# Two attentions with heads of eight numbers: scores of f32r parts in half of TensorE's rows, slots filled from SBUF

## The reference, cut to what matters

```python
# a1, causal
scores = einsum('bhqd,bhkd->bhqk', q, k) / sqrt(8)
scores = where(causal, scores, -inf)
o = einsum('bhqk,bhkd->bhqd', softmax(scores), v)      # then @ W_proj + b_proj
# b1, encoder: no mask, no scale, and a position bias that is added after the softmax
att = softmax(einsum('nqd,nkd->nqk', q, k))
att_out = einsum('nqk,nkd->nqd', att + batch_pos, v)   # then @ Wo.T + bo
```

## Time and profile before

| | us |
|---|---|
| three runs | 2855.39, 2871.22, 2868.68; median 2868.68 |
| profiled execution, its own time | 2866.75 |
| its span, first to last instruction | 2864.9 |
| its mean granted TensorE clock | 0.907 of 2.4 GHz |

### The profile page before, as it was taken

How to read it: one execution, slowest core, us unless ns; L and a number is a source line. 1 busy time by engine, 2 the same in 40 slices (tenths; PEclk the granted TensorE clock), 3 DMA queues, 4 the chain that set the end, 5 groups by cost and what they waited for, 6 DMA issues and landing times. The chain is left out here.

```text
span 2864.9 us, 41721 instructions
## 1 busy us (share of the span) xinstructions
PE 2471.5 (86%) x12332; PEld 1460.6 (51%) x12332; DVE 2117.8 (74%) x4148; ACT 1425.9 (50%) x3005; POOL 645.5 (23%) x621
## 2 busy tenths in 40 slices
PE   6994899939988999779996499999758899969998
PEld 4772344327756555457773422222125555437776
DVE  3994767538968999279995188788337899738998
ACT  2552356615520787246664036666611387615665
POOL 2334000013328000124444100000004500013443
PEclk7996799969979999889997769999978999979999
DMA  1213222012210000034442621211121000004443
GB/s 64 81 55 74 52 60 60 20 47 95 75 41 5 1 1 1 8 115 153 142 151 46 155 44 28 53 29 28 24 30 41 5 1 1 8 6 157 144 152 117
DMA packets 109527, 169.58 MB, mean 59 GB/s; under 512 B 58547, under 2 KB 80947, under 8 KB 98275
## 3 DMA queue, kind: packets, MB, share of 16 engines
q1 hardware_dynamic: 92468, 165.47, 19.5%
q10 hardware_dynamic: 16896, 2.10, 0.5%
HBM read 145.96 MB, written 12.78 MB: 55 GB/s over the span
## 5 line engine op out<-in xcount | busy, mean ns | idle before, releaser
L1483 DVE TENSOR_REDUCE b1x_maxima<-b1x_m_bank 128x1 f32<-128x512 f32 x512 | 317.9, 685 | 79.1 <-PE b1x_m_bank L1401 79.1
L1523 ACT ACTIVATE b1x_probs<-b1x_e_bank 128x1024 f32<-128x1024 f32 x256 | 248.3, 1022 | 117.4 <-PE b1x_e_bank L1419 117.2
L1483 DVE TENSOR_REDUCE a1x_maxima<-a1x_m_bank 128x1 f32<-128x512 f32 (+3 forms) x384 | 190.1, 551 | 73.1 <-PE a1x_m_bank L1404 49.3
L1401 PE MATMUL b1x_m_bank<-b1a_k_slot,b1a_q_slot 96*128 96x512 bf16 x512 | 190.8, 413 | 19.2 <-DMA b1x_v_slot<-b1a_v_aug 18.5
L1523 ACT ACTIVATE a1x_probs<-a1x_e_bank 128x1024 f32<-128x1024 f32 (+1 forms) x192 | 147.7, 809 | 102.4 <-PE a1x_e_bank L1422 80.1
L1419 PE MATMUL b1x_e_bank<-b1a_q_slot,b1a_k_slot 128*128 128x512 bf16 x512 | 154.1, 385 | 6.5 <-issue 3.9
L1435 PE MATMUL b1x_o_bank<-b1x_probs,b1x_v_slot 128*32 128x512 f32 x1024 | 137.4, 609 | 0.7 <-ACT b1x_probs L1523 0.7
L1401 PE MATMUL a1x_m_bank<-a1a_k_slot,a1a_q_slot 96*128 96x512 bf16 (+3 forms) x384 | 120.5, 351 | 19.9 <-DMA a1x_v_slot<-a1a_v_aug 18.6
L1401 PEld LDWEIGHTS b1x_m_bank<-b1a_k_slot,b1a_q_slot 96*128 96x128 bf16 x512 | 41.6, 98 | 177.2 <-DVE b1x_maxima L1483 126.2
L585 ACT ACTIVATE g1e_high<-g1e_hidden 128x512 fp32r<-128x512 f32 x128 | 81.1, 634 | 90.2 <-DVE g1e_hidden L618 90.1
L585 ACT ACTIVATE g2e_high<-g2e_hidden 128x512 fp32r<-128x512 f32 x128 | 81.2, 634 | 89.8 <-DVE g2e_hidden L618 89.6
(11 more groups left out here) (556 smaller groups left out, 6616.0 us busy)
## 6 DMA issues: line engine op xcount, KB each, us to landing
g1e_share<-scratch_combine SPq DMA_DIRECT2D x32, 1024.0 KB, 4.9
g2e_share<-scratch_combine SPq DMA_DIRECT2D x32, 1024.0 KB, 4.8
f1e_share<-scratch_combine SPq DMA_DIRECT2D x9, 1024.0 KB, 4.9
f2e_share<-scratch_combine SPq DMA_DIRECT2D x9, 1024.0 KB, 5.0
b1e_window<-scratch_bias_table SPq DMA_DIRECT2D x16, 320.0 KB, 4.8
a1a_k_slot<-scratch_k_parts SPq DMA_DIRECT2D x24, 192.0 KB
a1a_q_slot<-scratch_q_parts SPq DMA_DIRECT2D x72, 64.0 KB
b1a_k_slot<-scratch_k_parts SPq DMA_DIRECT2D x24, 192.0 KB
```

The lines of the kernel that those rows point to most:

```text
L1401: mm = pe.matmul(bank[:, 0:width], q_slot[s][0:MAX_ROW, qt // 4, hh, chunk(qt % 4, 128)], k_slot[s][0:MAX_ROW, hh, k0:k0 + width], start=T ...
L1483: dve.tensor_reduce(maxima[:, k0 // NC, col:col + 1], bank[:, 0:width], AX, ALU.max).then_inc(m_taken, 1)
L1523: act.activation(probs[g % 2][:, 2 * pair:2 * pair + 2, 0:width], e_bank[pair][:, :, 0:width], ACT.Exp, scale=scale).then_inc(exp_done, 1)
```

## The change

- Parts: two f32r parts (high, rest) instead of three bf16. A head takes 24 rows (q: high, rest, high; k: high, high, rest), zeros in q up to row 55, and the maximum's two parts in rows 56 and 57 against ones. Two heads lie in the two halves of the rows (0 and 64), two pairs beside each other in the free dimension. First-pass matmuls take 56 rows, second-pass scores 58, from row 0 or 64. Items run over the heads innermost, and the second pair's scores in the order 1, 0. The mask matmuls stay as they were (128 rows).
- Cutting: ACT writes the high part (one activation), DVE the rest (one scalar_tensor_tensor). No part goes to DRAM. `load` fills a slot with 2 x 4 x 3 DMAs from SBUF: groups 0 and 1 in earlier phases (a1: SP in q and in w; b1: SP in d, ACT's queue in e), group 2 at the start of x, later ones behind. The values are read from `v_aug` in place.
- POOL sets whole slots (k to 1.0, q to 0.0) in q, ahead of `v_aug`.
- Groups are unrolled. A plan `due(u)` gives the m items per unit by their columns; all turns stand six items behind their half. The rows' DMAs are 4 a half instead of 3, one half ahead (encoder) or two (causal).
- The encoder's q and k weights are permuted, so that a part's partition is (number, position).

The diff, cut to its core:

```diff
-PARTS = 3
+PARTS = 2
-MAX_ROW = 96
+MAX_ROW = 56
+SLOTS = 3
@@ class Narrow
+    ROW_PARTS = {"q": (0, 1, 0), "k": (0, 0, 1)}
+    LOADED = 16 * 2 * 4 * 3
+    def load(self, queue, group, operand):
+        parts, slot = ((self.q_parts, self.q_slot) if operand == "q" else (self.k_parts, self.k_slot))
+        s = group % SLOTS
+        for e in range(4):
+            b, n = (4 * group + e) // NH, (4 * group + e) % NH
+            for i, part in enumerate(self.ROW_PARTS[operand]):
+                if self.positions_split:
+                    src = parts[:, part, b * L + 64 * n:b * L + 64 * n + 64]
+                else:
+                    src = parts[HD * n:HD * n + HD, part, chunk(b, L)]
+                r = 64 * (e % 2) + HD * i
+                queue.dma_start(slot[s][r:r + HD, e // 2, :].bitcast(F32), src.bitcast(F32)).then_inc(self.slot_loaded[s], 16)
+    def prepare_slots(self, pool):
+        for s in range(SLOTS):
+            self.memset(pool, self.k_slot[s][:].bitcast(F32), 1.0)
+            self.memset(pool, self.q_slot[s][:].bitcast(F32), 0.0)
@@ qkv_in_parts: SP (a1), POOL, ACT, DVE
+                sp.wait_ge(narrow.set, 2)
+                sp.wait_ge(low_done, 4)
+                narrow.load(sp, 0, "q")
+                narrow.load(sp, 0, "k")
+            narrow.prepare_slots(pool)
             narrow.prepare_values(pool)
+                    act.activation(parts[m][:, 0, chunk(n)], acc[i % ROT][:], ACT.Identity,
+                                   bias=b[:, m:m + 1]).then_inc(high_done, 1)
+                dve.scalar_tensor_tensor(out=parts[m][:, 1, chunk(n)], in0=acc[i % ROT][:],
+                                         scalar=b[:, m:m + 1], in1=parts[m][:, 0, chunk(n)],
+                                         op0=ALU.add, op1=ALU.subtract).then_inc(low_done, 1)
@@ narrow_attention: the plan
+    for half in reversed(range(HALVES)):
+        items.insert(min(last_item[half] + 6, len(items)), (half, None))
+    AHEAD = 2 if causal else 1
+    worth = [0]
+    for item in items:
+        worth.append(worth[-1] + (item[4] + 32 if item[1] is not None else 256))
+    def due(u):
+        if u >= NU:
+            return NI
+        lead = turn_at[AHEAD - 1] + (8 if causal else 12)
+        done, whole = (sum(unit[3] + 32 for unit in units[:u]), sum(unit[3] + 32 for unit in units))
+        aim = worth[lead] + worth[NI] * done / whole
+        return max(m for m in range(NI + 1) if worth[m] <= aim)
@@ SP
+            narrow.load(sp, 2, "q")
+            rows(0)
+            narrow.load(sp, 2, "k")
+            for half in range(1, AHEAD):
+                rows(half)
+            for half in range(HALVES):
+                group = half // 2 + SLOTS - 1
+                if SLOTS <= group < GROUPS and half % 2 == 0:
+                    sp.wait_ge(pv_done, last_unit[half - 1] + 1)
+                    narrow.load(sp, group, "q")
+                    narrow.load(sp, group, "k")
+                if half + AHEAD < HALVES:
+                    rows(half + AHEAD)
+                store(half)
@@ PE: first_pass, scores
+                rows = slice(64 * (hh % 2), 64 * (hh % 2) + MAX_ROW)
+                mm = pe.matmul(bank[:, 0:width], q_slot[s][rows, hh // 2, chunk(qt, 128)],
+                               k_slot[s][rows, hh // 2, k0:k0 + width], start=True, stop=not diagonal)
                 if diagonal:
                     mm = pe.matmul(bank[:, width - 128:width], ident_bf[:], mask[:, 0, :],
                                    start=False, stop=True)
+                for a in ((0, 1) if pair == 0 else (1, 0)):
+                    rows = slice(64 * a, 64 * a + MAX_ROW + PARTS)
+                    mm = pe.matmul(e_bank[pair][:, a, 0:width], k_slot[s][rows, pair, chunk(kt, 128)],
+                                   q_slot[s][rows, pair, lo:lo + width], start=True, stop=not diagonal)
                     if diagonal:
                         mm = pe.matmul(e_bank[pair][:, a, 0:128], ident_bf[:], mask[:, 1, :],
                                        start=False, stop=True)
```

More of the change, by code:

```diff
@@ L1105, in prepare_values @@
         self.memset(pool, self.v_heads[:, :, :, :, HD], 1.0)
[L1107 to L1115, removed]
 def qkv_in_parts(nc, tag, dram, narrow, h, early, name, v):
     ROT = 6
[L1128 to L1131, removed]
+    items = [(2, n) for n in range(NCH)] if v is not None else []
+    VALUES = len(items)
+    items += [(m, n) for n in range(NCH) for m in range(2)]
     with Phase(nc, tag) as p:
@@ L1267, in narrow_attention @@
         block = p.block()
[L1268 to L1282, removed]
+        heads_out = dram["heads_out"]
         @block.sync
@@ L1372, in _ @@
-            rows(0, 0)
-            def step(it, j, group, last):
-                if not last:
-                    rows(group + 1, (j + 1) % 3)
-            over_groups(pool, step)
-        def count(group, per, index):
-            return group * per + index
+            for half in range(HALVES):
+                into = max_parts[half % 2]
+                pool.wait_ge(m_taken, turn_at[half] + 1)
+                if half >= 2:
+                    pool.wait_ge(rows_set[half % 2], 64 * (half // 2))
+                pool.tensor_copy(into[:, 0, :], rest[:]).then_inc(cut, 1)
+                pool.wait_ge(cut, 2 * half + 1)
+                pool.tensor_tensor(into[:, 1, :], rest[:], into[:, 0, :], ALU.subtract).then_inc(cut, 1)
@@ L1472, in m_item @@
-            def m_item(group, s, m):
-                item = items[m]
-                dve.wait_ge(m_done, count(group, NM, m + 1))
-                bank = m_bank[(s * NM + m) % 3]
-                if item[0] == "turn":
-                    dve.wait_ge(cut, group * (2 * CUT) + item[1] * CUT + CUT)
+            for m in range(NI):
+                half, qt = items[m][0:2]
+                qh = half % 2
+                dve.wait_ge(m_done, m + 1)
+                bank = m_bank[m % 3]
+                if qt is None:
+                    if half >= 1:
+                        dve.wait_ge(cut, 2 * half)
@@ L1543, in _ @@
-            over_groups(act, step)
+            exponentials(0)
+            for u in range(NU):
+                half = units[u][0]
+                if u + 1 < NU:
+                    exponentials(u + 1)
+                if u == last_unit[half]:
+                    act.wait_ge(pv_done, u + 1)
+                    if half >= 2:
+                        act.wait_ge(o_stored[half % 2], 64 * (half // 2))
+                    act.activation(o_sb[half % 2][:], o_bank[:], ACT.Copy).then_inc(o_copied, 1)
```

368 lines of the change are left out of this document (119 added, 249 removed).

## The result

The changed kernel takes 3132.05 us (median of 4 runs, 3127.92 to 3135.48) against 2864.41 of the kernel before beside it: ratio 1.094, interval 1.0909 to 1.097. It is slower, as forecast, but by 268 us and not by 120; the time lies above the range. The profiled execution took 3135.48 us, span 3133.6, 268.7 more than that of before.

The account below looks back on a forecast made before the run. PE (TensorE), busy 86% of the span, was taken to bound the kernel. From 2866.75 us, +202 (a1x), -55 (b1x), -21 and -8 (ahead of them) gave 2985; range 2860 to 3090.

Parts of the forecast that it names:

- The price of a trip: On PE, going between full and half rows and back costs 0.31 us at 2.4 GHz, about 0.44 at 1.2.
- a1x at full clock: Causal attention a1x goes from 285.8 to 403 us (+117), with +159 from 512 trips at the masks.
- The clock in a1x: In a1x a third of the work runs at 1.2 GHz, +85 us, making a1x 488.
- The bound of two thirds: Upper bound for a1x: two thirds at the low clock, +287 us, and 20 more if f32r is slower at 128 columns.
- b1x's unit: In encoder attention b1x, PE needs 2.06 us a unit, under DVE's 2.39; with extras and slack the unit is 2.55.
- The rows in b1x: In five groups of b1x, SP's 24 slot DMAs delay the rows DMAs, costing 8 us.
- Ahead of the stretches: Phases before b1x and a1x shorten, mainly since slots are filled earlier: -21 us and -8 us.
- A: Rival: shape changes are free or hidden, so packing wins everywhere; a1x -53 us, time 2730, chance 0.15.
- C: Rival: half of the trip is hidden and the clock holds; a1x +37 us, time 2820, chance 0.09.
- B: Rival: trips cost 0.31 us but the clock holds through a1x; a1x +117 us, time 2900, chance 0.14.
- D: Rival: the row halves don't run together; b1x's unit is 2.94 us, time 3055, chance 0.02.
- DVE's idle near nothing: Sign in b1x that the forecast is right: DVE hardly idles, with units of 2.5 to 2.6 us.

Follow-up runs that it names:

- experiment 5: Kernel after with each of the 512 causal mask matmuls issued four times in a row, all trips kept: 3069.21 us, ratio 1.0721.
- experiment 7: Kernel after with one first-pass item instead of two ahead of the values, encoder only: 3188.49 us in a single run.
- Experiments 4 and 6: Against the kernel after: 4, rows DMAs ahead of slot loads, 3118.52 us; 6, that plus half-row masks and one unit more encoder lead, 2850.13 us.

## Why the prediction was wrong

The mechanism was right, and so was the sign. The sum missed 150 us: 100 in a1x, 46 in b1x, the rest ahead of them.

- **The price of a trip: right.** 0.32 and 0.40 us for 0.31 and 0.44, and at 2.4 GHz also in its parts: 0.10 and 0.11 for the two changes of shape and 0.11 for a weight load in the open, for 0.09, 0.09 to 0.10 and 0.11 read from the earlier trace rows.
- **a1x at full clock: right.** By the estimate from experiment 5 a group takes 48.7 for 32.0 us, +16.7; the forecast's +117 over eight groups is +14.7. For the whole stretch: the clock's 0.56 means that some 88% of the 587.4 us were at the lower level, where work takes 77.6 / 48.7 = 1.59 times as long, so it would be 517 / 1.59 + 70 = 395 us. The forecast had 403.
- **The clock in a1x: the step that failed.** "With a third of the work at 1.2 GHz ... +85". Measured: 587.4 - 395 = 192 us. Not a third but some four fifths of the work ran at 1.2 GHz (517 / 1.59 = 325 of 395 us, an estimate, since the 48.7 is one). The price for such work was about right: 85 us for a third would be 210 for 0.82 of it. In one group of the trace not a microsecond was at 2.4 GHz. I had expected the clock to come back among the full-width units without masks; it did so for 3.4 to 17 us at a time. The third was a guess about lengths, and no row gave it: the earlier trace rows have a stretch with PE busy 1.90 of 3.40 us ahead of a fall and one with 32.79 of 36.00 at 1.00, but also one with 32.86 of 34.00 at 0.50, so the busy share could not tell which way a1x would go. The bound of two thirds (+287) was passed, and +301.6 is under +307 only by the 20 us for slower f32r, which did not come.
- **b1x's unit:** "PE unit under DVE's 2.39, unit 2.55" assumed that the later of two engines sets the pace. The loop of three banks does, at 2.70 (experiment 7): 117 x 0.15 = 18 us of the 46 to 50 missed. The last item's 0.42 (2005.06 to 2005.48, for 0.21 of columns) belongs to this loop too: its weight load starts only at 2005.06, when its bank is free, so the load lies in the open beside the change of shape.
- **The rows in b1x:** priced at 8 us. Experiments 4 and 6 took out 5 to 13 (rows behind the loads) and about 15 more (the chain from turn to rows was later than the lead in every half, not in five groups). Left is 382.8 against the 352 of the forecast without this term: the unit's 18, a unit of 3.30 at the start of each half, 15 x 0.6 = 9, in which ACT also copies the output bank (read from the order of time, not tested), and 4 that I can't place. The forecast said b1x -55; it was -8.5.
- **Ahead of the stretches: right.** -18.1 and -6.5 for -21 and -8; the slots in SBUF give what they should.
- **The rivals.** A and C are out by the trips, B by the clock, D by the pairs. "DVE's idle near nothing" was a wrong sign to look for.

The forecast's rule on the upper bound was sound, but the range stopped at the sum of a1x's bound and my point values for b1x; b1x's miss carried the time past it.

## What to carry to other kernels

Here packing paid only once everything that is interleaved had the packed shape: bring masks, biases and transposes into it (here twice 64 rows for once 128) before counting the gain. Price the clock as a state of a whole stage, at both levels, and don't read it from the busy share. After a change that makes a stage faster, look again at each queue that feeds it: the same order on SP was free at 72 us a group and cost 35 us in all at 33.

## What the runs showed that I had not expected

- More matmuls took less time twice: 1536 matmuls added to the kernel after, -63 us (3132.05 to 3069.21); 1024 added to the kernel without masks, a1x from 307.6 to 295.7.
- PE's clock stood at 1.2 GHz for 77.6 us while the profile showed PE busy for 99.5% of it. The Trainium skill, "TensorE: Matmul & The Clock Gate", section HAM oscillation, lays such a fall to gaps in which PE idles; PE's only wait in this stretch was 0.4 us, so here that is not enough as an explanation. Experiment 5 kept every trip, added columns, and had 1.00.
- A change between full and half rows costs 0.10 to 0.13 us in either direction and at either clock. What makes the trip dear beyond the two changes is that the f32r score's weight load starts only with the score: 0.11 us at 2.4 GHz, 0.17 at 1.2 (0.30 less 0.13).
- f32r matmuls of 128 columns show no slower rate: at 1.2 GHz 128, 256 and 512 columns are followed by the mask 0.40, 0.51 and 0.72 us later, 0.29 or 0.30 beyond their columns each. The 20 us held for four passes in the bounds were not needed.
